# The maxima's row in a transformer layer on one core: two DMA issues by SyncE, or one by SyncE and one by ScalarE

## The reference

```python
q = (x @ wq.T).reshape(b, s, N_HEADS, HEAD_DIM)          # k, v alike
scores = einsum('bihd,bjhd->bhij', q, k) * scale
scores = where(j - i > WINDOW // 2, -inf, scores)
attn = softmax(scores, axis=-1)
out = einsum('bhij,bjhd->bihd', attn, v).reshape(b, s, d) @ wo.T
x = x + out
z = layernorm(x)
x = x + (silu(z @ gate_w.T) * (z @ up_w.T)) @ down_w.T
```

## Time and profile before

| what | value |
|---|---|
| median of 3 runs | 533.26 us (532.91 to 536.58) |
| the profiled execution's own time | 533.84 us |
| its span on the core | 532.1 us |
| granted TensorE clock, mean over the span | 0.99 |
| busy: TensorE / VectorE / ScalarE / GpSimd | 506.1 / 425.0 / 364.8 / 212.4 us |

### The profile page before, as it was taken

The page is one execution under the profiler, slowest core; times in us unless marked ns, Lnnn a source line. Parts: engine busy times, 40 slices in busy tenths (PEclk is TensorE's granted clock), DMA queues, the critical chain, the costliest instruction groups (busy, mean ns, idle before and its releaser), DMA issues.

```text
span 532.1 us, 12740 instructions
## 1 busy us (share of the span) xinstructions
PE 506.1 (95%) x4840; PEld 434.8 (82%) x4840; DVE 425.0 (80%) x944; ACT 364.8 (69%) x536; POOL 212.4 (40%) x255
## 2 busy tenths in 40 slices
PE   6997979999999999999999999999999998999986
PEld 4676757898888898888888888988888887879776
DVE  3675778798888989898988989888897886786853
ACT  2367778586767878686877778786868765765622
POOL 4675343524334342424333433424252434324413
PEclk9799999999999999999999999999999999999999
DMA  8553432123211313131222113131232102110001
GB/s 267 167 176 109 127 104 80 62 73 108 93 50 40 120 63 120 61 121 62 99 72 82 55 66 111 62 121 60 82 121 80 56 8 81 56 45 22 22 1 40
DMA packets 45500, 44.51 MB, mean 84 GB/s; under 512 B 4736, under 2 KB 44544, under 8 KB 45440
## 3 DMA queue, kind: packets, MB, share of 16 engines
q1 hardware_dynamic: 45440, 43.70, 25.0%
HBM read 13.01 MB, written 4.19 MB: 32 GB/s over the span
## 4 chain that ended last, share of the span: by engine, by line
PE 75%; DVE 8%; SPq 6%; ACT 4%; issue 3%; DMA 2%; POOL 1%; POOLq 0%; DVEq 0%; ACTq 0%
PE ring L959 9%; PE ring L1037 7%; PE ring L961 7%; PE ring L960 7%; PE pair L1029 6%; PE pair L1014 6%; PE ring L1068 6%; PE ring L1069 4%; PE ring L1070 4%; PE ring L952 3%; SPq L651 3%; PE ring L1057 2%; PE ring L943 2%; SPq L637 2%; PE ring L954 2%
## 5 line engine op out<-in xcount | busy, mean ns | idle before, releaser
L787 ACT ACTIVATE P<-pair 128x800 f32<-128x800 f32 x128 | 106.8, 838 | 45.4 <-PE pair L1029 35.0
L883 DVE TENSOR_REDUCE M<-pair 128x2 f32<-128x288 f32 (+1 forms) x256 | 133.5, 565 | 5.2 <-PE pair L1014 5.1
L721 POOL TENSOR_TENSOR IN<-GU,IN 128x512 fp32r<-128x512 f32 x64 | 82.9, 1296 | 132.9 <-ACT IN L726 132.6
L726 ACT ACTIVATE pair<-SEED 128x800 f32<-128x800 bf16 x128 | 107.7, 842 | 11.0 <-DVE M L883 7.0
L713 POOL TENSOR_SCALAR_AFFINE_SELECT P<-P 128x448 f32<-128x448 f32 x64 | 37.5, 585 | 116.6 <-ACT P L787 116.6
L1068 PE MATMUL ring<-Y,WGUh 128*128 128x256 f32 x256 | 76.5, 299 | 1.3 <-DVE Y L828 1.2
L959 PE MATMUL ring<-WD,IN 128*128 128x256 f32 x256 | 76.5, 299 | 0.9 <-POOL IN L721 0.8
L1069 PE MATMUL ring<-Y,WGUh 128*128 128x256 f32 x256 | 72.0, 281 | 0.0
L1070 PE MATMUL ring<-Y,WGUl 128*128 128x256 f32 x256 | 71.8, 280 | 0.0
L960 PE MATMUL ring<-WD,IN 128*128 128x256 f32 x256 | 71.5, 279 | 0.0
L961 PE MATMUL ring<-WD,IN 128*128 128x256 f32 x256 | 71.5, 279 | 0.0
(11 more groups left out here) (94 smaller groups left out, 1169.5 us busy)
## 6 DMA issues: line engine op xcount, KB each, us to landing
QM<-QK SPq DMA_DIRECT2D x96, 128.0 KB, 2.1
KS<-QK SPq DMA_DIRECT2D x96, 128.0 KB, 2.1
X<-x SPq DMA_DIRECT2D x32, 256.0 KB, 3.0
out<-X SPq DMA_DIRECT2D x16, 256.0 KB, 2.2
OVERD<-over_down SPq DMA_DIRECT2D x2, 512.0 KB, 5.9
PO<-W SPq DMA_DIRECT2D x16, 48.0 KB, 2.2
P<-wqk SPq DMA_DIRECT2D x2, 256.0 KB, 5.7
QM<-MT SPq DMA_DIRECT2D x32, 8.0 KB
```

The lines of the kernel that those rows point to most:

```text
L726: copy = lambda dst, src: nc.scalar.activation(dst, src, ACT.Copy)
L787: nc.scalar.activation(P[:, g % 2, 2 * (n % 2):2 * (n % 2) + 2, :], pair(what, t, n)[:, :, 0:SW], ACT.Exp, scale=SCALE).then_inc(exp_done, 1)
L883: i = nc.vector.tensor_reduce(out=M[:, t % 2, it, :].rearrange("p (a k) -> p a k", a=2)[:, :, n], in_=pr[:, :, cols], axis=AX.X, op=ALU.ma ...
```

## The change

In step `mt` SyncE issues only the first of the two DMAs. ScalarE gets a branch for `mt`: it waits for VectorE's copy, as SyncE does, and issues the second DMA from its own queue. Sources, targets, sizes and the semaphore with its count of 32 for each turn are the same. No other step is touched, and the table of the order is the same.

```diff
                 elif what == "mt":
                     sp.wait_ge(mt_done, nth("mt", t, 0))
-                    for a in range(2):
-                        r = STACK * a + STACK - 1
-                        sp.dma_start(QM[r:r + 1, t % 2, :, :].bitcast(F32),
-                                     MT[a * NP:(a + 1) * NP, :].bitcast(F32)).then_inc(m_loaded[t % 2], DMA)
+                    sp.dma_start(QM[STACK - 1:STACK, t % 2, :, :].bitcast(F32),
+                                 MT[0:NP, :].bitcast(F32)).then_inc(m_loaded[t % 2], DMA)
...
+                elif what == "mt":
+                    act.wait_ge(mt_done, nth("mt", t, 0))
+                    nc.scalar.dma_start(QM[2 * STACK - 1:2 * STACK, t % 2, :, :].bitcast(F32),
+                                        MT[NP:H, :].bitcast(F32)).then_inc(m_loaded[t % 2], DMA)
```

## The result

The changed kernel takes 561.84 us (median of 4 runs, 561.51 to 566.43), against 533.5 for the one before beside it: ratio 1.0563, 95% interval 1.0526 to 1.0600. It is 28 us slower. The forecast was 19 us slower, 552.4 us, and its range ended at 561.0. The profiled execution took 561.51 us, its span is 559.9 us (532.1 before) and its mean granted clock 0.974 (0.99 before).

The account below looks back on a forecast made before the run. PE was taken to bound the kernel, busy for the whole 29.45 us period. Stalls 19.7 plus turn 2's 0.8 less the win of 1.4 gave +19.1 on 533.26, 552.4 us; range 544 to 561.

Parts of the forecast that it names:

- The stalls of `dn` 0: PE's `dn` 0 starts late behind ScalarE's wait and issue, about 2.3 us in most of nine turns, 19.7 us in all.
- The issue on ScalarE: Time ScalarE spends issuing the DMA ahead of the `ic` 1 copy: 0.69 us, bounds 0 and 1.4.
- The rival of an issue at 1.4: Simultaneous issues on SyncE and ScalarE hold each other up: 558.6 us, or 560 with turn 2 at its bound; chance 0.12.
- the one of a free issue: The issue costs ScalarE nearly nothing, only the wait for the cast remains: +12.2, 545.5 us; chance 0.13.
- The sum over the period: PE has no idle time in its 29.45 us period, so any wait of PE is added to the turn.
- Turn 5 and turn 2: Turn 5: `dn` 0 late by 1.48 us. Turn 2: late tanh and gate delay PE's gate matmuls 0.8, bounds 0 and 2.0.
- The terms put at nought: Turns 0, 1, 4: ScalarE arrives after the cast; turns 3, 15: tanh late about 1 us or less; no cost.
- The win: Second DMA issued up to 0.73 us earlier, shortening PE's waits in turns 0 and 1 by 0.7 each, 1.4 in all.
- Two transfers to disjoint halves: By the skill's rule the two DMAs serialize, so the 1.4 us would not come and the sum be 1.4 higher.

Follow-up runs that it names:

- issue_only: The kernel before, plus a 4 KB DMA of constants to scratch, issued by ScalarE at the `mt` step without any wait: 533.67 us, ratio 1.0024.
- wait_only: The kernel before, with ScalarE only waiting for the cast at the `mt` step and SyncE issuing both DMAs: 547.57 us, ratio 1.0292.
- keep_busy: The changed kernel, plus 14 unused matmuls on constants ahead of `dn` 0 in nine of the ten stalled turns: 558.99 us, ratio 1.0485.
- one_dma: The kernel before, with one 16 KB DMA on SyncE in place of the two of 8 KB: 529.67 us; timed again, 528.63 us.
- past_one: The changed kernel, but ScalarE's issue one step later in turns 5 to 15, two in turn 2: 530.94 us; again (`_b`) on another chip, 530.34 us.

## Why the prediction missed

The direction, the place and the size of the stalls were right; the time came out 9.4 us above the forecast and 0.8 us outside the range.

- **The stalls of `dn` 0.** Ten stalls came where they were forecast. Forecast in turns 5 to 13: 19.7 us net. Measured from the profile's gaps in turns 5 to 14: 20.5 us, of which turns 13 and 14 swallowed the waits of 0.40 and 1.98 that stood behind the earlier trace rows, which leaves 18.1, with the gaps some 0.15 short each. Right, but by luck in turn 14. The wait of 1.98 there, which the forecast let swallow the stall, belonged to the one execution that was profiled: the second row landed 3.72 us after its issue, against 1.92 to 2.14 in the other turns. In the profile of issue_only, where SyncE issues both DMAs as before, it landed after 1.96, and PE didn't wait for it. Against such an execution the stall of turn 14 costs its 1.9 us.
- **The issue on ScalarE.** Taken at SyncE's 0.69, bounds 0 and 1.4; measured 0.63, and two issues released at the same instant ran side by side (284.43 and 284.44). The rival of an issue at 1.4 is out, and so is the one of a free issue, as long as a wait stands before it. wait_only against the changed kernel prices it in the stall at 0.74. (Nine turns at 1.4 instead of 0.69 cost 6.4 more, not the 6.2 of the prediction.)
- **The sum over the period: the step that failed.** "Whatever makes PE wait anywhere in a turn is added to the turn" counted the wait and nothing else. The bill had a second item, PE's clock after the wait. Four stretches at 1.2 GHz behind the stalls cost 1.5 us each, 6 us, and keep_busy took exactly that off the steady periods. A fifth, in turn 1, is 1.5 us more, but also appears in one_dma and past_one_b, where no stall of ScalarE's making precedes it, and not in wait_only, where the stretch near 50 lasts 6.83 us instead. The executions of the unchanged kernel vary in the same way: the 23 timed beside wait_only had mean clocks from 0.979 to 0.990, which by 0.003 a stretch is an estimate of up to three more than in the profile of before (0.990). So it is taken as chance; no run switched it on or off.
- **It could have been read before.** The kernel before already had such a stretch, and the prediction never looked at the clock by windows. Two windows of its trace, behind the same columns as above:

```profile
47.60:50.90 3.30, 0.80 (x11) 0.63 (x10) 0.94 (x2) 1.55 (x3) 2.41 (x2) 1.00 0.48 137
51.00:54.30 3.30, 3.30 (x18) 2.94 (x18) 1.16 (x5) 2.17 (x3) 1.84 (x3) 0.50 0.57 193
```

  PE waited 1.80 and 0.70 us in the first and was granted half the clock in the second, though it was busy throughout there. With nine stalls of 2.3 us in view, up to nine such stretches at 1.5 us belonged into the upper bound: 552.4 + 13.5, about 566.
- **Turn 5 and turn 2.** In turn 5 the stall was 1.29, but two waits at the next scores, for VectorE and for ScalarE, cost 0.46 more. Turn 2 was taken at 0.8; its two new waits, these, make 1.2:

```profile
98.87 0.38 PE L1070 MATMUL ring<-Y,WGUh 128*128 128x256 f32 x1 [0.40 <-DVE GU L926]
...
103.03 0.39 PE L1016 MATMUL pair<-KS,QM 63*128 63x256 f32 x2 [0.82 <-ACT pair L724]
```

  The terms put at nought (the tanh in turns 3 and 15) showed no stall of PE behind them, but for one of 0.26 in turn 15 (512.30) that the kernel before doesn't have.
- **The win.** Forecast 1.4 in turns 0 and 1. The rows of the changed kernel that answer to the first of the earlier trace rows:

```profile
48.15 0.39 PE L1031 MATMUL pair<-QM,KS 64*128 64x256 f32 x2 [1.08 <-DMA QM<-MT]
...
71.42 0.39 PE L1031 MATMUL pair<-QM,KS 64*128 64x256 f32 x2 [1.60 <-DMA QM<-MT]
```

  1.80 became 1.08, and 1.96 became 1.60: 1.1 us. past_one shows the win without the cost, 1.3 to 2.7 us.
- **Two transfers to disjoint halves.** In turn 8 of past_one both DMAs were issued at 271.48, and the last count of `m_loaded` came at 273.77, 2.29 us later. Before, the second's last count came 1.95 us after its own issue (274.21 to 276.16). So issued together they land about 0.3 us later than that, and 0.4 of the 0.73 is won. In turns 0 and 1 it is otherwise: there SyncE comes to its issue 2.0 us after ScalarE, and the last row lands 2.0 us after SyncE's issue, so that in turn 0 all of the 0.73 was won. The Trainium skill ("DMA: Bandwidth & Descriptors", section "Rules for kernel authors") says that such transfers serialize and advises a single one in their place. The traces agree only in part: 2.27 us for both together is far from twice 1.95. The single transfer, one_dma, was the fastest kernel.

Account of the 27.8 us between the two spans: stalls 20.5 less the 2.4 that they swallowed, turns 2 and 5 1.7, five stretches of lower clock 7.5, win -1.1. That is 26.2. The rest, 1.6, is about what the ten gaps are short of (ten times 0.15). The busy times on the two pages agree with this: PE's idle time grew from 26.0 us to 44.5, by 18.5 (stalls, turns 2 and 5 and the win make 18.7), and its busy time by 9.3, of which 7.5 are the five stretches.

## What to carry to other kernels

A DMA issue put on a compute engine's queue is cheap where it has nothing to wait for, and it costs the whole wait where it has: look up what stands behind it on that queue, who waits for that, and with how much slack, and move the issue to where the engine would be idle anyway. When TensorE is the bound, price a new stall of it with the granted clock behind it, by windows of the trace that already have such a stall. Before splitting two small DMAs over two queues, try to make them one.

## What the runs showed of the hardware

- ScalarE's queue issued a DMA while the engine ran a tanh: issue 270.72 to 271.35, tanh 270.71 to 271.31 (issue_only).
- An issue of 8 rows took ScalarE 0.63 us and SyncE 0.69; one DMA of 16 rows into two took SyncE 0.55.
- Two DMAs of 8 KB issued at the same instant from SyncE and ScalarE had both landed after 2.27 us (median, past_one), one of 16 KB after 1.94 (one_dma). Now and then one landed late: 3.72 us after its issue in turn 14 of before, 4.06 in turn 3 of past_one_b.
- Stalls of TensorE of 1.4, 2.1 and 2.8 us, once each turn with the engine busy throughout between them, were followed by 3.4 us at 1.2 GHz in 0, 4 and 8 of ten turns, in one profiled execution each; each such stretch cost about 1.5 us. Which of several equal stalls is hit, the runs do not explain.
